# A two-layer decoder block: the last layer's attention values read from PSUM, and other orders of work on four engines

## What is computed

```python
def l1_attn(x, W_Q, W_K, W_V):                    # per token; no token sees another
    Q, K, V = ((x @ W.T).reshape(B, L, 16, 16) for W in (W_Q, W_K, W_V))
    sK = softmax(swapaxes(K, -1, -2), axis=-1)    # 16 x 16 for each token
    tran_V = einsum('bldh,blhe->blde', sK, V)
    return einsum('blhd,blde->blhe', softmax(Q, -1), tran_V).reshape(B, L, d)

def l1_xattn(x, context, ...):                    # 16 heads over 64 context rows
    xn = layernorm(x) * gamma + beta
    return softmax(xn @ Wq @ k.T * scale + mask) @ v @ Wo + bo

def l1_ffn(x, ...):                               # 256 -> 1024 -> 1024 -> 1024 -> 256
    h = silu(x @ w1) * (x @ w2)
    h = gelu(h @ h1); h = gelu(h @ h2)
    return h @ w3

x = layernorm(x + l0_ffn(x))                      # x3
x = layernorm(x + l1_attn(x))                     # x4
x = layernorm(x + l1_xattn(x, ctx))               # x5
x = layernorm(x + l1_ffn(x))
```

## Time and profile before

| | |
|---|---|
| median of three runs | 1385.09 us (1380.93 to 1385.64) |
| the profiled execution | 1375.68 us, its span 1374.1 us |
| granted TensorE clock, whole span | 0.913 |
| busy, share of the span | PE 78%, DVE 69%, ACT 39%, POOL 28% |
| the last layer | from about 673 us to the end |
| starts of `first` on PE, pairs 0 to 7 | 784.26, 858.52, 934.45, 1011.97, 1087.84, 1165.41, 1241.47, 1318.40 |
| four pairs in the steady part | 873.24 to 1180.13 us |

### The profile page before, as it was taken

The page is one execution under the profiler, slowest core; times in us unless marked ns, Lnnn a source line. Parts: engine busy times, 40 slices in busy tenths (PEclk is TensorE's granted clock), DMA queues, the critical chain, the costliest instruction groups (busy, mean ns, idle before and its releaser), DMA issues. The chain is left out here.

```text
span 1374.1 us, 20926 instructions
## 1 busy us (share of the span) xinstructions
PE 1073.3 (78%) x6765; PEld 894.1 (65%) x6770; DVE 951.4 (69%) x1785; ACT 538.5 (39%) x1562; POOL 389.4 (28%) x525
## 2 busy tenths in 40 slices
PE   1588988866676789999524699888888888887887
PEld 1477777744165578888403477777777768776787
DVE  5689999855856112222299998989899898989321
ACT  0112121122054422322102374766655765756553
POOL 1112222100013400000320153636363443636232
PEclk9799999987788689999867799999999999999999
DMA  8015530000000966666270000000000000000000
GB/s 282 16 69 177 180 100 8 1 1 1 0 1 31 368 234 247 223 226 235 78 323 9 1 1 1 9 0 4 4 0 8 0 8 0 8 0 8 0 9 9
DMA packets 23974, 98.88 MB, mean 72 GB/s; under 512 B 3728, under 2 KB 15184, under 8 KB 17584
## 3 DMA queue, kind: packets, MB, share of 16 engines
q1 hardware_dynamic: 16080, 73.60, 14.5%
q10 hardware_dynamic: 5200, 17.37, 3.8%
q0 software_dynamic: 2640, 7.21, 1.5%
HBM read 87.96 MB, written 21.76 MB: 80 GB/s over the span
## 5 line engine op out<-in xcount | busy, mean ns | idle before, releaser
L1997 PE MATMUL bank<-n_hA_hi_reduced,ffn_h 128*128 128x256 f32 x512 | 126.4, 290 | 9.2 <-POOL n_hA_lo_reduced L1820 5.8
L1997 PE MATMUL bank<-n_hB_hi_reduced,ffn_h 128*128 128x256 f32 x512 | 127.9, 293 | 1.5 <-DVE n_hB_lo_reduced L2334 1.5
L1997 PE MATMUL bank<-n_hA_lo_reduced,ffn_h 128*128 128x256 f32 x512 | 123.4, 284 | 0.0
L1997 PE MATMUL bank<-n_hB_lo_reduced,ffn_h 128*128 128x256 f32 x512 | 123.4, 285 | 0.0
L1997 PEld LDWEIGHTS bank<-n_hA_hi_reduced,ffn_h 128*128 128x128 f32 x512 | 99.7, 195 | 11.0 <-POOL n_hA_lo_reduced L1820 10.5
L1614 ACT ACTIVATE e_hT<-bank,e_b 128x128 f32<-128x128 f32 x184 | 52.5, 368 | 135.7 <-PE bank L1557 135.7
L1997 PEld LDWEIGHTS bank<-n_hB_hi_reduced,ffn_h 128*128 128x128 f32 x512 | 100.2, 196 | 3.3 <-issue 3.3
L2248 DVE TENSOR_TENSOR d_prod<-d_qk,d_xT 128x512 f32<-128x512 f32 x128 | 101.9, 836 | 0.5
L1997 PEld LDWEIGHTS bank<-n_hB_lo_reduced,ffn_h 128*128 128x128 f32 x512 | 100.0, 195 | 1.7 <-issue 1.7
L1997 PEld LDWEIGHTS bank<-n_hA_lo_reduced,ffn_h 128*128 128x128 f32 x512 | 99.6, 195 | 0.2
L1639 DVE TENSOR_TENSOR e_y<-bank,e_b 128x256 f32<-128x256 f32 x23 | 9.8, 425 | 123.7 <-PE bank L1569 123.7
(11 more groups left out here) (344 smaller groups left out, 2674.2 us busy)
## 6 DMA issues: line engine op xcount, KB each, us to landing
e_w<-in_W SPq DMA_DIRECT2D x23, 1024.0 KB, 5.0
ffn_weights<-in_F ACTq DMA_DIRECT2D x2, 5632.0 KB, 20.7
e_piece<-ffn_weights SPq DMA_DIRECT2D x11, 1024.0 KB, 4.9
ffn_h<-ffn_weights SPq DMA_DIRECT2D x2, 4096.0 KB, 18.7
ffn_w<-ffn_weights SPq DMA_DIRECT2D x3, 1024.0 KB, 6.6
expert_rows<-zero ACTq DMA_DIRECT2D x1, 2944.0 KB, 10.3
e_xs<-expert_rows SPq DMA_DIRECT2D x23, 128.0 KB, 4.5
expert_out<-e_y POOLq DMA_DIRECT2D x23, 128.0 KB, 2.0
```

The source lines that it names most:

```text
L1997: last = nc.tensor.matmul(F[f % 2][:, 0:PAIR], weight(w[:, k, f * P:(f + 1) * P], fast), operand(src[part][1][:, k, :], fast), start=(c == ...
```

## The change

Three parts.

1. The copy `v_copied` is gone. `contexts` reads V out of its bank. V has a PE step of its own, `projected_v`, which waits until the tile before has been read (`v_read`); Q and K are announced before it. The transposed x3 goes into the upper half of `bank_o`, the bank of `summed`, instead of `bank_v`, with the waits that guard that.
2. The lists `trip(n)` of PE, ACT, DVE and POOL have other orders. One `qk_exp` of ACT now stands between two units of hidden 2, which makes nine table loads a trip of what were eight.
3. In the opening the two powers stand after 4 and 8 gathers, not after 6 and 12.

The diff, cut to its core; of the lists only the pieces that the text speaks of:

```diff
-    vs = [t[:, :, :].rearrange("p k (e h) -> p (k e) h", h=H) for t in xT]
+    values = bank_v[:, 0:D].rearrange("p (e h) -> p e h", h=H)
...
                 if not (isinstance(n, int) and n < 2):
                     tile(x_powered, n, 0)
+                pair(lower_parts, n - 3, 1, 2, 8)
+                tile(out_powered, n - 2, 1)
+                row_of(added, n - 3, 0)
                 tile(attn_powered, n - 1, 0)
                 if isinstance(n, int) and n == 1:
                     x_powered(2, 1, 0)
-                pair(gated_product, n - 2, 0, 2)
+                tile(x5_kept, n - 2, 1)
...
-                if t == 3:
+                if t == 2:
                     x_powered(0, 0, 0)
-                elif t == 6:
+                elif t == 4:
                     x_powered(1, 0, 1)
...
             def turned_x3(k, i, b):
                 pe.wait_ge(q["x3"], k + 1)
-                after("v_copied", k)
+                after("x3T", k)
+                after("out_var", k - 2)
                 for c in range(KD):
-                    last = nc.tensor.transpose(bank_v[:, D + c * P:D + (c + 1) * P], x3[b][:, c * P:(c + 1) * P],
+                    last = nc.tensor.transpose(bank_o[:, D + c * P:D + (c + 1) * P], x3[b][:, c * P:(c + 1) * P],
                                                m.ident[:, :])
                 last.then_inc(q["x3_turned"], 1)
 
             def qkv(k, i, b):
                 pe.wait_ge(q["x3T"], k + 1)
                 after("pre", k)
-                for lo, hi, to in ((0, 2 * D, bank_qk), (2 * D, 3 * D, bank_v)):
-                    for c in range(KD):
-                        last = nc.tensor.matmul(to[:, 0:hi - lo], xT[b][:, c, :], m.wqkv1[:, c, lo:hi],
-                                                start=(c == 0), stop=(c == KD - 1))
+                for c in range(KD):
+                    last = nc.tensor.matmul(bank_qk[:, 0:2 * D], xT[b][:, c, :], m.wqkv1[:, c, 0:2 * D],
+                                            start=(c == 0), stop=(c == KD - 1))
                 last.then_inc(q["qkv_done"], 1)
+
+            def projected_v(k, i, b):
+                pe.wait_ge(q["x3T"], k + 1)
+                after("v_read", k)
+                for c in range(KD):
+                    last = nc.tensor.matmul(bank_v[:, 0:D], xT[b][:, c, :], m.wqkv1[:, c, 2 * D:3 * D],
+                                            start=(c == 0), stop=(c == KD - 1))
+                last.then_inc(q["v_done"], 1)
...
             def summed(k, i, b):
                 pe.wait_ge(q["probT"], k + 1)
                 after("out_var", k)
+                pe.wait_ge(q["x3T"], min(k + 3, NT) if isinstance(k, int) else k + 3)
...
                 tile(turned_x3, n, 0)
                 tile(qkv, n, 0)
+                tile(projected_v, n, 0)
                 pair(hidden, n - 2, 0, 0, 2, fast)
                 tile(turned_probs, n - 1, 0)
-                pair(hidden, n - 2, 0, 2, 7, fast)
+                pair(hidden, n - 2, 0, 2, 5, fast)
                 tile(summed, n - 1, 0)
+                pair(hidden, n - 2, 0, 5, 7, fast)
                 tile(turned_xn, n - 1, 1)
                 pair(hidden, n - 2, 0, 7, 8, fast)
+                tile(scores, n - 1, 1)
+                pair(hidden, n - 2, 1, 0, 1, fast)
                 tile(turned_x3, n, 1)
-                tile(scores, n - 1, 1)
-                pair(hidden, n - 2, 1, 0, 3, fast)
+                pair(hidden, n - 2, 1, 1, 4, fast)
                 tile(turned_x5, n - 1, 0)
-                pair(hidden, n - 2, 1, 3, 5, fast)
+                pair(hidden, n - 2, 1, 4, 5, fast)
                 tile(qkv, n, 1)
+                pair(hidden, n - 2, 1, 5, 6, fast)
+                tile(projected_v, n, 1)
                 tile(turned_probs, n - 1, 1)
-                pair(hidden, n - 2, 1, 5, 8, fast)
+                pair(hidden, n - 2, 1, 6, 8, fast)
                 tile(summed, n - 1, 1)
                 row_of(final, n - 2, 0, fast)
+                tile(turned_x5, n - 1, 1)
                 row_of(final, n - 2, 1, fast)
-                tile(turned_x5, n - 1, 1)
-                pair(first, n - 1, 0, 4, fast)
+                pair(first, n - 1, 0, 2, fast)
                 tile(turned_xn, n, 0)
-                pair(first, n - 1, 4, 8, fast)
+                pair(first, n - 1, 2, 8, fast)
...
-            def v_copied(k, i, b):
-                act.wait_ge(q["qkv_done"], k + 1)
-                nc.scalar.activation(vs[b][:, :, :].rearrange("p a b -> p (a b)"), bank_v[:, 0:D],
-                                     ACT.Copy).then_inc(q["v_copied"], 1)
...
                 act.wait_ge(q["xn_turned"], k + 1)
+                act.wait_ge(q["v_done"], k + 1)
...
                 tile(score_exp, n - 1, 1)
-                pair(hidden, n - 2, 1, 3, 4)
+                pair(hidden, n - 2, 1, 4, 5)
                 tile(x5_copied, n - 1, 0)
-                tile(v_copied, n, 1)
-                pair(hidden, n - 2, 1, 4, 6)
+                pair(hidden, n - 2, 1, 5, 6)
                 tile(probs_copied, n - 1, 1)
-                pair(hidden, n - 2, 1, 6, 8)
+                pair(hidden, n - 2, 1, 6, 7)
+                tile(qk_exp, n, 1)
+                pair(hidden, n - 2, 1, 7, 8)
                 tile(x5_copied, n - 1, 1)
-                tile(qk_exp, n, 1)
...
                 kn = groups(qk[b][:, D:2 * D])
-                v.wait_ge(q["v_copied"], k + 1)
+                v.wait_ge(q["v_done"], k + 1)
                 to = T.rearrange("p e d -> p d e")
                 products(4 * quarter, 4 * quarter + 4, quarter == 3,
                          lambda at, n: V.tensor_tensor(part[n], spread(kn[:, at:at + TWO, :], 2, DH),
-                                                       spread(vs[b][:, :, :], 1, TWO), ALU.mult),
+                                                       spread(values, 1, TWO), ALU.mult),
                          lambda at, n: V.tensor_reduce(to[:, at:at + TWO, :], part[n], AX.X, ALU.add))
+                if quarter == 3:
+                    v.sem_inc(q["v_read"], 1)
...
                 tile(contexts, n - 1, 0, 3)
-                tile(probabilities, n - 2, 1)
                 tile(attended, n - 1, 0, 0)
                 tile(attended, n - 1, 0, 1)
-                tile(x5_split, n - 2, 0)
+                tile(probabilities, n - 2, 1)
                 tile(attended, n - 1, 0, 2)
+                tile(prepared, n - 1, 1)
                 tile(attended, n - 1, 0, 3)
                 tile(out_summed, n - 2, 1)
-                tile(prepared, n - 1, 1)
+                tile(x5_split, n - 2, 0)
                 tile(x5_normed, n - 2, 1)
+                tile(attention_summed, n - 1, 0)
+                tile(x5_split, n - 2, 1)
...
                 tile(attention_summed, n - 1, 1)
                 tile(prepared, n, 0)
+                tile(out_summed, n - 1, 0)
                 tile(x4_and_xn, n - 1, 1)
+                tile(x5_normed, n - 1, 0)
```

66 lines of the change are left out of this document (28 added, 38 removed).

## The result

The changed kernel takes 1376.43 us at the median of four runs (1374.72 to 1378.58), the kernel before 1385.2 in the same comparison: a ratio of 0.994, with a 95% interval from 0.9922 to 0.9958. It is faster, but by 0.6%, 9 us, where 33 us and 1352 were forecast; the time lies outside the range of 1334 to 1374.

The account below looks back on a forecast made before the run. DVE was taken to bound the last layer, PE close behind. Six periods -25.8, opening -2.5 and drain -5 made -33.3 us: 1342.4 profiled, 1352 as forecast median; own range 1343 to 1360, 8-in-10 range 1334 to 1374.

Parts of the forecast that it names:

- The products: First attention on DVE: 16 products a pair fall from 865 to 692 ns each, 2.77 us off a pair.
- The rival of the dear bank: DVE products with a bank operand carry a fixed extra cost, 8 to 65 ns each: 1353 to 1358 us; chance 0.05.
- The wait for the exponentials: DVE's wait for ACT in the second attention: 2.6 of 3.0 us a pair go, 0.4 stays.
- The wait for the sum over values: DVE's wait for PE's sum after the probabilities: about 1.9 us instead of 1.19, priced at +0.8 a pair.
- The PE side of the sum: PE's waits for the probabilities and the copy of values give at most 4.85 us a pair; -4.3 taken.
- The opening: Start of the last layer: earlier powers and announced Q and K gain 4.2 us, slow sums reduce it to -2.5 net.
- The drain and the tail: Last full period: bounds 0 and -9.5 us, -5 taken; what follows it unchanged.
- It does nothing net: Rival for the whole kernel: DVE's gain is given back by PE's order, 1385 us; chance 0.06.
- only one half of it works: Rival: products stay slowed, or DVE's wait moves, for instance to the sum over values; 1364 us; chance 0.18.
- The V projection never blocked PE: Rival: PE's V projection waits for the tile before and holds up work queued behind it; 1395 us; chance 0.07.
- The warning in the forecast's last sentence: Forecast fails most easily if sum-over-values waits exceed 2 us or PE's clock falls in new waits; no price or chance.

Follow-up runs that it names:

- the filled kernel: The changed kernel with PE running the hidden unit just ahead of each turn of the probabilities twice, to fill its two stalls; 1361.11 us, ratio 0.9832.
- the values alone: The kernel before with values read from the bank, V projection its own step, x3 turned into the other bank, old orders and opening; 1379.41 us, ratio 0.9961.
- the orders alone: The changed kernel with the values copied to SBUF by ACT again, keeping the new orders, separate V projection and opening; 1384.48 us, ratio 0.9991.

## Why the prediction was wrong

**The products.** Right: 0.692 us priced, 0.680 measured, and none of them over 0.690 with POOL at work. The rival of the dear bank falls. By the Trainium skill, "VectorE: DVE Perf Modes", section "The TRN2 errata", the bank form would have been an estimated 65 ns longer than the 684 of the earlier trace rows; the measurement decides against it. In agreement is a rule of the Trainium skill, "SBUF — State Buffer", section "Who interferes with whom": a DVE instruction with two inputs in SBUF contends with a GpSimd instruction that reads SBUF; with one of them moved to a bank the 0.18 us went. `attended`, which still has two, takes 794 ns (768 before).

**The wait for the exponentials.** Right: 0.72 us a pair is left (0.4 forecast).

**The wait for the sum over values.** This is the step that failed. The forecast was 8.2 us on PE from the turn to the sum's end, 6.3 on DVE beside it, and a wait of 1.9. With the clock held the filled kernel shows 8.21 (996.00 to 1004.21) and a wait of 1.71: the step is right for PE at full clock. In the changed kernel it is 9.81 (1003.65 to 1013.46) and 3.87. The term had PE's durations at the clock of the earlier trace rows in a place where PE had just stood still for 2 us, and I had seen the same in the trace of before and left it out: the clock is 0.98 over the four pairs there, not 1.00, and 0.58 over the 4 us from the turn of one of them, ahead of which PE stood still for 2.12 us:

```profile
995.42:999.50 4.08, 4.08 (x22) 4.08 (x23) 4.08 (x7) 1.76 (x6) 1.91 (x2) 0.58 0.00 0
```

The term was mis-sized at its other end as well. The 1.19 us that it starts from is the longest wait of before, not the mean:

```profile
DVE d_r L2296 <- PE bank L1944: 2.6, 3, 1.2
```

That is 0.65 us a pair. So the wait grew by 2.7 us a pair (3.35 - 0.65), where +0.8 was forecast.

**The PE side of the sum.** I let both of PE's waits go, 4.85 us a pair at most. The one for the copy of the values went. The one for the probabilities grew from 13.1 to 18.0 us in four pairs. The first tile's probabilities now come behind two quarters of `attended` instead of one, and behind moments of the output, a piece of DVE's list that the diff above leaves out:

```diff
                 tile(attended, n - 1, 1, 0)
+                row_of(y_moments, n - 3, 0)
+                tile(attended, n - 1, 1, 1)
                 tile(probabilities, n - 1, 0)
                 row_of(y_moments, n - 3, 1)
                 row_of(y_normed, n - 3, 0)
-                tile(attended, n - 1, 1, 1)
```

So the first turn has a stall of 2.4 us in each pair, where it had none to 1.58 us; with the values alone it stayed at 1.46 to 1.58, with the orders alone it became 3.12 to 3.23. Behind each of these first stalls, and behind three of the four second ones, the clock fell. Filled, the pair takes 72.39 us, against a forecast of 72.4; unfilled 75.08. The gain of 4.4 us a pair was there to be had, and 2.7 of it was given back by the clock. That the filled pair meets the forecast so closely is luck in part: DVE's busy time fell by 3.7 us a pair and its idle time by 0.7, where 2.8 and 1.1 were forecast, and 0.4 was added to get between DVE and PE.

**The opening.** The powers were priced rightly (2.5 on the first tile: 5.46 us after the gather instead of 7.95; 2.85 in all). What I left out is that the first two trips have no hidden units, so that the probabilities' later place and the wait of the V projection lie open there: +1.2 us instead of -2.5. That the values cost the opening 1.6 was measured; that it is by these two waits is argued.

**The drain and the tail.** The last full period fell by 2.3 us, 76.93 to 74.60 (forecast 5). What follows grew by 1.05, 55.70 to 56.75 (forecast 0); the cause of that stays open.

**The sum.** Opening +1.2, six periods -6.0 (451.25 us instead of 457.21), drain -2.3, tail +1.05: -6.1 by the traces, where -33.3 was forecast, and -8.8 by the medians. The six periods miss by 19.8 us, most of all. The lower end of the forecast's own range, 1343, doesn't follow from -5.3 us a pair, which gives 1346.

**The rivals.** None of them was this one. "It does nothing net" lies nearest in time (1385 us), by a gain that PE's order gives back; "only one half of it works" (1364) named the wait that moves to the sum over values. Both left out the clock. The V projection never blocked PE in the steady part. The warning in the forecast's last sentence, a clock that falls in waits that are new, is what happened; it should have been a rival with a price: up to two falls a pair, 1.6 us each.

## What to carry to other kernels

Where an engine that is nearly full stands still for a moment and its own speed depends on that, its durations from an undisturbed stretch are not the price of the work behind the stall; take them from behind a stall of that length. When two engines wait for each other in turn, look whether a cheaper step on one only moves the wait. If a stall of PE can't be removed, useless matmuls in it, in a place where their result is overwritten or unread, can be worth more than the work moved: here 15 us of 1376, and 24 with the opening filled too and the last pair left unfilled. That holds only where the work behind the stall is on the path: in the kernel before the same filling gained nothing, and elsewhere in the changed kernel the same work cost 3.7 us a pair.

## What the runs showed of the hardware

PE's clock can fall after a stall of only 2.1 to 2.4 us in the middle of dense work: behind a stall of 2.40 us the granted clock was 0.80 over the 7.0 us of hidden units that followed the turn, behind one of 2.13 us it was 0.75 over 5.1. It is not the length alone that decides. In the four pairs of the changed kernel the clock fell behind all four stalls of 2.4 us and behind three of the four of 2.13; with the first of them filled, behind one of four of 2.12 to 2.18. In the kernel with the orders alone it stayed at 1.00 behind stalls of 3.12 and 3.04 us. The Trainium skill, "TensorE: Matmul & The Clock Gate", section "HAM oscillation — how this bites in real kernels", describes a kernel in which each wait between bursts of matmuls brings the clock down again; the trace agrees in part: 1.6 us are lost at each fall, but not each wait brings one.

A 128x512 DVE product with one operand in a bank takes 680 ns beside POOL's work, against 865 with both operands in SBUF and 684 for that form where POOL adds nothing up.
